# The patches' squares: weighted on ScalarE and summed on VectorE instead of by matmuls, and the embedding's order in the queue

## What is computed

```python
# embedding: the picture and four copies shifted by a pixel, in 16 x 16 patches
xs = jnp.concatenate([x] + [_shift(x, s) for s in shifts], axis=1)
t = xs.reshape(B, C5, h, PATCH, w, PATCH).transpose(0, 2, 4, 3, 5, 1).reshape(B, h * w, PATCH * PATCH * C5)
mu, var = jnp.mean(t, -1, keepdims=True), jnp.var(t, -1, keepdims=True)
h = jnp.einsum('bnp,pd->bnd', (t - mu) * jax.lax.rsqrt(var + EPS) * ln_gamma + ln_beta, W) + b
h = jnp.concatenate([h, txt], axis=1)               # 196 patches + 128 words = 324 tokens of 192
h = h + attention(layernorm(h))                     # 12 heads of 16, rotary, causal, a sink column
h = h + experts(layernorm(h))                       # 64 slots, softmax over tokens and over slots
```

## Time and profile before

| | |
|---|---|
| median of 3 runs | 3160.82 us (3148.11 to 3165.07) |
| the profiled execution's own time | 3153.97 us |
| its span | 3152.2 us |
| mean granted clock of TensorE | 0.944 |
| TensorE busy (matmul) | 2757.7 us, 87% |
| TensorE busy (weight load) | 1983.3 us, 63% |
| VectorE | 1720.3 us, 55% |
| ScalarE | 1599.8 us, 51% |
| GpSimd | 1067.5 us, 34% |

### The profile page before, as it was taken

The page is one execution under the profiler, slowest core; times in us unless marked ns, Lnnn a source line. Parts: engine busy times, 40 slices in busy tenths (PEclk is TensorE's granted clock), DMA queues, the critical chain, the costliest instruction groups (busy, mean ns, idle before and its releaser), DMA issues. The chain is left out here.

```text
span 3152.2 us, 71273 instructions
## 1 busy us (share of the span) xinstructions
PE 2757.7 (87%) x24706; PEld 1983.3 (63%) x24706; DVE 1720.3 (55%) x7720; ACT 1599.8 (51%) x3234; POOL 1067.5 (34%) x1877
## 2 busy tenths in 40 slices
PE   3069999999999999999999999999999997577856
PEld 3057777777777777777777777777777775344432
DVE  2436666666666666666666666666666664111123
ACT  0036666666666666666666666666666654100000
POOL 2134444444444444444444444444444441000000
PEclk8579999999999999999999999999999997688888
DMA  3333333333333333333333333333333321899979
GB/s 104 49 92 89 92 95 94 91 93 92 91 91 93 96 96 94 97 93 97 95 94 93 95 94 93 94 92 94 91 91 91 92 76 36 206 270 271 255 210 308
DMA packets 368820, 361.12 MB, mean 115 GB/s; under 512 B 32479, under 2 KB 339756, under 8 KB 368205
## 3 DMA queue, kind: packets, MB, share of 16 engines
q1 hardware_dynamic: 344332, 339.13, 39.9%
q10 hardware_dynamic: 24128, 17.42, 1.8%
HBM read 196.51 MB, written 43.25 MB: 76 GB/s over the span
## 5 line engine op out<-in xcount | busy, mean ns | idle before, releaser
L961 DVE CUSTOM_DVE_ANT_0 ps<-ps,late 128x325 f32<-128x325 f32 (+2 forms) x2304 | 748.4, 396 | 7.6 <-PE ps L606 4.0
L813 ACT ACTIVATE prob<-ps 128x590 f32<-128x590 f32 x768 | 501.5, 661 | 183.2 <-PE ps L629 168.4
L563 PE MATMUL ps<-window_w,xp 108*98 108x193 f32 x2304 | 498.7, 335 | 107.3 <-ACT xp L813 107.3
L563 PEld LDWEIGHTS ps<-window_w,xp 108*98 108x98 f32 x2304 | 336.9, 166 | 110.4 <-ACT xp L813 107.4
L606 PE MATMUL ps<-kst,qst 99*128 99x325 bf16 (+2 forms) x2304 | 330.1, 253 | 38.3 <-DVE negmax L961 31.8
L1144 POOL TENSOR_TENSOR rot<-by_cos,by_sin 96x324 f32<-96x324 f32 x128 | 111.8, 873 | 685.9 <-DVE by_sin L1056 685.9
L770 PE MATMUL ps<-xt,wqk 97*96 97x324 f32 (+1 forms) x1024 | 321.0, 446 | 1.7 <-ACT xt L813 1.7
L961 DVE DVE_READ_ACCUMULATOR2_ANT negmax<- 128x1 f32 (+1 forms) x2304 | 318.1, 138 | 0.0
L606 PEld LDWEIGHTS ps<-kst,qst 99*128 99x128 bf16 (+1 forms) x2304 | 199.4, 106 | 183.5 <-DVE negmax L961 136.5
L645 PE MATMUL ps<-prob,vaug 128*32 128x324 f32 (+2 forms) x4608 | 286.2, 340 | 0.0
L1043 DVE RECIPROCAL rden<-ps 98x12 f32<-98x12 f32 (+1 forms) x192 | 43.4, 226 | 385.2 <-PE ps L789 385.2
(11 more groups left out here) (178 smaller groups left out, 5636.5 us busy)
## 6 DMA issues: line engine op xcount, KB each, us to landing
w<-in_L_ffn_fc_weight_dram SPq DMA_DIRECT2D x128, 576.0 KB, 11.7
xw<-in_x_dram SPq DMA_DIRECT2D x384, 189.0 KB
qst<-part SPq DMA_DIRECT2D x768, 60.8 KB
kst<-part SPq DMA_DIRECT2D x768, 60.8 KB
h_held<-h_new SPq DMA_DIRECT2D x64, 288.0 KB, 3.7
residual_image<-h SPq DMA_DIRECT2D x64, 147.0 KB
h_i<-residual_image SPq DMA_DIRECT2D x16, 588.0 KB
out_dram<-h_i ACTq DMA_DIRECT2D x32, 294.0 KB
```

The source lines that it names most:

```text
L563: mm = pe.matmul(ps[0:TILE, BK7, half * (D + 1):(half + 1) * (D + 1)], xp[:, q, TILE * half:TILE * (half + 1)], window_w[:, q, :], start=( ...
L813: return nc.scalar.activation(out_, in_, f, **kw)
L961: last = dve.tensor_tensor_reduce(out=ps[0:nq, bk, col:col + keys], in0=ps[0:nq, bk, col:col + keys], in1=late[0:nq, gone:gone + keys], sc ...
```

## The change

The squares of a patch are formed otherwise. GpSimd once makes `root` = the square root of the pixel weights. ScalarE squares with a scale: (root * x)^2, in five activations, one for each distinct set of weights (q = 0, 1, 2 to 6, 7, 8). VectorE sums `xsq` over q in one `tensor_reduce` whose input is read in the order (patch, q), so elements 784 bytes apart; it stands between `dmax` and the copy of the second maxima. TensorE keeps the two small products that add the partitions. The nine strip products and ScalarE's copy of them go. `EMBED_AT` puts all 18 embedding products in the maxima phase.

```diff
-EMBED_AT = [0, 5, 1, 0, 2, 0, 0, 0, 1, 0, 0, 4,
-            1, 1, 1, 1, 1, 0, 0, 0, 0, 0, 0, 0]
+EMBED_AT = [0, 5, 1, 1, 2, 1, 1, 1, 1, 1, 1, 3,
+            0, 0, 0, 0, 0, 0, 0, 0, 0, 0, 0, 0]
...
+                        pool.memset(half_power[:], -0.5)
+                        pool.tensor_scalar(root[:], window_w[:, :, D], 1e-30, 0.0, ALU.max, ALU.add)
+                        pool.drain()
+                        pool.tensor_tensor(root[:], root[:], half_power[:], ALU.pow)
+                        pool.drain()
+                        pool.tensor_tensor(root[:], root[:], window_w[:, :, D], ALU.mult)
...
-                    def square_strips(b, columns):
...
                     def square_sums(b):
-                        strips_ready.wait(pe, b)
+                        sq_summed.wait(pe, b)
                         for half in range(2):
                             col = 2 * (D + 1) + half
-                            mm = pe.matmul(ps[0:TILE, BK7, col:col + 1], strips[:, TILE * half:TILE * (half + 1)],
-                                           per_strip[:], start=True, stop=True)
+                            mm = pe.matmul(ps[0:TILE, BK7, col:col + 1], sq_sum[:, TILE * half:TILE * (half + 1)],
+                                           ones[:], start=True, stop=True)
...
-                            if front and h in (5, 6):
-                                square_strips(b + 2, range(4) if h == 5 else range(4, WIN2))
...
-                        if front:
-                            strips_mm.wait(act, b + 2)
-                            squares_mm.wait(act, b + 1)
-                            fn(strips[:], ps[:, BK4, 0:PATCHES], ACT.Copy).then_inc(strips_ready.sem, 1)
...
-                            strips_mm.wait(act, b + 2)
+                            sq_summed.wait(act, b + 2)
                             act.drain()
-                            fn(xsq[:], xp[:], ACT.Square).then_inc(sq_ready.sem, 1)
+                            for q0, q1 in ((0, 1), (1, 2), (2, 7), (7, 8), (8, 9)):
+                                last = fn(xsq[:, q0:q1], xp[:, q0:q1], ACT.Square, scale=root[:, q0:q0 + 1])
+                            last.then_inc(sq_ready.sem, 1)
...
+                        if front:
+                            sq_ready.wait(dve, b + 2)
+                            squares_mm.wait(dve, b + 1)
+                            dve.tensor_reduce(sq_sum[:], xsq[:].rearrange("p q n -> p n q"), AX.X, ALU.add
+                                ).then_inc(sq_summed.sem, 1)
```

More of the change, by code:

```diff
@@ L317, in early_fusion_kernel @@
                 xp = tmp("xp", [2 * ROWS, WIN2, PATCHES])
-                strips, per_strip = tmp("strips", [128, PATCHES]), tmp("per_strip", [128, 1])
+                sq_sum, ones = tmp("sq_sum", [2 * ROWS, PATCHES]), tmp("ones", [2 * ROWS, 1])
+                root, half_power = tmp("root", [2 * ROWS, WIN2]), tmp("half_power", [2 * ROWS, WIN2])
                 xsq = tmp("xsq", [2 * ROWS, WIN2, PATCHES])
@@ L389, in early_fusion_kernel @@
                 max_in = [Signal(f"max_in{g}", 16) for g in range(2)]
-                embed_mm, strips_mm, squares_mm, xt_mm, v_mm, yt_mm, proj_mm = (
-                    Signal(n, 1) for n in ("embed_mm", "strips_mm", "squares_mm", "xt_mm", "v_mm", "yt_mm", "proj_mm"))
+                embed_mm, squares_mm, xt_mm, v_mm, yt_mm, proj_mm = (
+                    Signal(n, 1) for n in ("embed_mm", "squares_mm", "xt_mm", "v_mm", "yt_mm", "proj_mm"))
                 zt_mm, l_mm, lt_mm, ct_mm, d_mm, ym_mm = (
@@ L400, in early_fusion_kernel @@
                     Signal(n, 3) for n in ("pv_mm", "yr_mm"))
-                sq_ready, strips_ready, xt_ready, v_ready, yt_ready, zt_ready, zs_ready = (
-                    Signal(n, 1) for n in ("sq_ready", "strips_ready", "xt_ready", "v_ready", "yt_ready", "zt_ready", "zs_ready"))
+                sq_ready, sq_summed, xt_ready, v_ready, yt_ready, zt_ready, zs_ready = (
+                    Signal(n, 1) for n in ("sq_ready", "sq_summed", "xt_ready", "v_ready", "yt_ready", "zt_ready", "zs_ready"))
                 l_scaled, ce_ready, de_ready, ct_ready, ym_ready = (
@@ L441, in _ @@
                         dve.memset(zero[:], 0.0)
-                        dve.memset(per_strip[:], 1.0 / STRIP)
+                        dve.memset(ones[:], 1.0)
                         for t in (lmax, lsum, mrest, rstd2):
```

## The result

The changed kernel takes 3184.59 us (median of 8 runs, 3171.11 to 3205.21), the kernel before 3161.51 in the same comparison (8 runs): ratio 1.009, 95% interval 1.0055 to 1.0126. The forecast was 3139 us and faster. It came out 0.9% slower, inside the range of 3110 to 3192 and by the mechanism of the first rival.

A forecast was written before the change was run, and what follows sets the result against it. VectorE was taken to pace the maxima phase, TensorE to be last from head 6's load to the step's end. Terms +0.14 - 0.32 - 0.15 = -0.33 us a step, over 64 steps -21 us from 3160.8: 3139 us, range 3110 to 3192.

The forecast's parts named there:

- the first rival: VectorE's reduce pays for its 784-byte steps, taking 2.76 to 3.74 us and delaying second maxima and head 6; chance 0.30.
- the reduce's term: VectorE's strided reduce between `dmax` and the second maxima's copy: 1.98 us, at 1.04 ns an element plus 0.14 fixed.
- the 2.43 from which the copy is late: Reduce length in us above which the second maxima's copy delays ScalarE's DMA issue.
- the prediction's own formula: Second maxima's DMA issue falls at 1038.23 + r, r being the reduce's length; the issue before was at 1040.84.
- threshold of 2.76 us: Reduce length above which the step was predicted to lose time.
- the rule that I weighed lower than a row: Trainium skill's 1.73 ns for a hop at every element: reduce 3.2 us, +0.4 us a step, 26 us slower.
- Crowded slot 7: Embedding added behind head 7's scores in the maxima phase makes head 9 start 0.14 us later, on the path.
- Embedding off the path: Embedding behind head 2 in the exponential phase goes: head 3, fourth exponential and DMA issue come 0.32 us earlier.
- Landing: Second maxima's DMA lands about 2.3 us after issue; head 6 starts then instead of about 2.45 after: -0.15 us.
- that rival: The second maxima's landing never binds head 6: -0.79 us a step, 3110 us; chance 0.05.
- `xsq` 0.6 to 0.8 us longer: ScalarE's squares in five pieces grow from 1.67 us by this, hidden by 1.2 us of cover before GpSimd needs `part[0]`.
- TensorE as the bound of the maxima phase: Embeddings in slots 7, 9 and 10 each push VectorE, up to 0.5 us a step returns, about 3160 us; chance 0.13.

The follow-up runs named there:

- e8: Changed kernel plus VectorE scalings and reduces of 1764 elements timed in its setup: reduce 1.99 us in order, 3.28 hopping 784 bytes; scaling 1.08 us in order.
- e10: Changed kernel plus VectorE scalings timed in its setup: hopped at 64 bytes, 96 elements start 0.15 us apart, 196 elements 0.24; 784 take 0.82 us.
- e5: Changed kernel, embedding products behind maxima-phase heads 7 and 9 moved behind heads 0 and 1 of the exponential phase: ratio 1.0027 to the kernel before.
- e4: Kernel before, strips kept, only the table changed so that all embedding products stand in the maxima phase: 3121.38 us, ratio 0.9887.
- e9: Kernel of e5 with squares laid out by patch, so the reduce reads the right squares in order: 3138.25 us, ratio 0.9908 to the kernel before.
- e1: Changed kernel with the reduce reading squares in the order they lie, which sums wrong squares for each patch: ratio 0.9941 to the kernel before.
- e3: Changed kernel with four in-place adds over runs of neighbours instead of the reduce: 3324.45 us, ratio 1.0525 to the kernel before.
- e6: Changed kernel with the four adds of e3 and the embedding table of e5: ratio 1.0055 to the kernel before.
- e7: Kernel before, only the table changed as in e4, but two embedding products left behind heads 0 and 1 of the exponential phase: ratio 0.9910.

## Why the prediction was wrong, and where it was right

The step that failed is the price of the hop in the reduce's term: the sentence "a hop there costs no more than 1.04 ns an element with 0.05 us fixed", and with it "I take 1.98"; the reduce took 3.34 us. The row was right and its reading wrong, in two ways. The instructions of the earlier trace rows are scalings, and I compared their rate with the reduce's in-order rate. A scaling needs 0.53 ns in order (e8); at the 0.9 ns that e10 gives it when hopped, it was already paying 1.7 times. The setup of the kernel before has scalings in order too, and I did not put them beside (VectorE's timeline):

```profile
44.06 0.93 DVE L247 TENSOR_SCALAR wa<-wa,ns 96x576 f32<-96x576 f32 x2
```

That is at most 0.81 ns an element with the fixed parts in it, below the 1.04 that I took for "no slower than in order". And 0.15 us between starts bounds an element only by 0.15 / 96 = 1.56 ns, unless one knows the fixed part, which I took from nowhere in these rows; 1764 x 1.56 is 2.75 us, which is above the 2.43 from which the copy is late.

With 3.34 in the prediction's own formula, the issue falls 1041.57 - 1040.84 = +0.73 us later and the step gains back 0.15 at the landing: +0.58. Measured, the issue came 0.43 later after `dexp` and `dexp` 0.15 later in the step, the landing gave 0.19 back, and the ordinary step lost 0.44. So the formula around r holds to 0.15 us, and its threshold of 2.76 us gives the sign; only the r put into it was wrong. The Trainium skill (Vector Engine (DVE) Microarchitecture Reference, Measured stream behaviour on trn2) has 1.73 ns for a source that hops at every element; the reduce measured (3.28 - 0.15) / 1764 = 1.77 ns in e8, and runs of nine cost nothing, as the page has it for runs of two and more. For this reduce the rule that I weighed lower than a row was right.

The other terms:
- Crowded slot 7: +0.14 worked out; 13.40 to 13.55 measured, and 13.27 with slots 7 and 9 relieved (e5). Right.
- Embedding off the path: 0.32; 0.38 measured (e4). Right.
- Landing: 2.3 us after the issue; 2.27 in the step shown of e4, 2.26 on average in the changed kernel. Right. Head 6 never came before it; that rival is out.
- `xsq` 0.6 to 0.8 us longer, covered by 1.2: it takes 2.51 in place of 1.67, +0.84, a little over the bound, and GpSimd starts its split without waiting. Right in effect; e9 shows the cover's edge.
- TensorE as the bound of the maxima phase: VectorE waits 0.2 us a step, no more. Out.
- Not in the prediction at all: the clock. I had read 1.00 in rows 1 and costed idle time on TensorE at nothing. It cost the profiled execution of the changed kernel 0.2 to 0.3 us a step on average: its mean interval (39.07) lies 0.27 over its middle one (38.80), against 0.08 before.

Of 0.63 us in a step, then, 0.15 are the crowded slot, 0.43 the late issue, less 0.19 from head 6 taking the DMA at its landing; about 0.2 goes with the clock, and some 0.05 I can't place. e1, with the reduce in order, came to 0.9941 (0.9909 to 0.9972) where the forecast's 21 us would have been 0.993: with the hop's price right, the rest of the sum holds.

## What to carry to other kernels

Price a strided read by the same operation, once in order and once hopped. A short instruction of another kind, with another in-order rate, says little; and a start-to-start time bounds the rate only with nothing taken off for a fixed part. Where squares or sums can be laid out so that the reduce reads runs, it costs its plain rate (1.97 us in e9). The hops then move to another engine: measure the cover behind it there, and what the engines beside it do when it runs longer. Products on TensorE that only fill a wait can be worth their place (e5). The largest gain here came from the order of the queue alone, with the strips left as they were: once no embedding product stood between head 2 and head 3, where ScalarE waited for TensorE, the kernel was 1.1% faster (e4).

## What the runs showed that I had not expected

- TensorE's clock, at 2.4 GHz throughout the steady part before, fell to 1.2 GHz in some steps of the kernels in which it idled more. Busy 2.02 of 3 us came before a fall in the changed kernel, but 2.00 of 3 without one in another step, and e1 had 2.05 with one long step in 49; 1.28 of 3 came before a fall in e3, where nearly every step had one. Two embedding products of 0.33 us each, put into the wait, left one long step of ten (e5), and in e6 three of 43, with the table as the only difference to e3. Not every kernel with less on TensorE there lost clock: e4, e7 and e9 had no long step.
- VectorE's adds of two SBUF operands and GpSimd's operations held each other up: 1.23 us in place of 0.23 for 18 elements on GpSimd (e6), and 0.86 in place of 0.40 on VectorE for a `z` under GpSimd's `by_cos` (e9). The reduce, with its one source, did not hold GpSimd up.
- The sum by adds is thus no gain here: 2.5 us on VectorE in place of 3.3, and the same late issue.
